# Attention kernel, one core: the order of score pairs from a table of words, and other first steps

## The reference, cut to what matters

```
q, k, v = (x @ Wqkv.T + bqkv) split into 16 heads
attn = softmax(q k^T / 4)
coh  = sigmoid(tanh([x, c] @ Wc1.T + bc1) @ Wc2.T + bc2)
mod  = attn * coh / (sum(attn * coh) + 1e-8)
mod  = 0.79 * mod + 0.21 * fa            (fa: softmax over tokens, one row per batch)
x    = x + (mod @ v) @ Wout.T + bout
out  = x + quaternion_map(x)             (linear in x, per feature group)
```

## Time and profile before

| | |
|---|---|
| median of 3 runs | 289.14 us (288.78 to 289.9) |
| the profiled execution | 288.7 us, its span 286.8 us |
| PE busy | 266.9 us, 93% |
| DVE busy | 193.1 us, 67% |
| ACT busy | 176.3 us, 61% |
| POOL busy | 177.4 us, 62%, nearly all of it before 132 us |
| chain that ended last | PE 78%, DVE 16%, issue 3% |

### The profile page before, as it was taken

The page is one execution under the profiler, slowest core; times in us unless marked ns, Lnnn a source line. Parts: engine busy times, 40 slices in busy tenths (PEclk is TensorE's granted clock), DMA queues, the critical chain, the costliest instruction groups (busy, mean ns, idle before and its releaser), DMA issues.

```text
span 286.8 us, 4339 instructions
## 1 busy us (share of the span) xinstructions
PE 266.9 (93%) x1579; PEld 128.1 (45%) x1579; DVE 193.1 (67%) x219; ACT 176.3 (61%) x214; POOL 177.4 (62%) x162
## 2 busy tenths in 40 slices
PE   8999979989799999999999999999999788899963
PEld 7447533334344444445444544455444333362422
DVE  6377867776776767776777677766877688763223
ACT  3334357666777676766587686755677767656760
POOL 4993999999999999994030599991000899600000
PEclk9999999999999999999999999999999999999999
DMA  6813411521710020146600000335500001011002
GB/s 220 255 74 115 180 41 56 186 93 32 263 41 0 5 71 3 61 185 215 231 9 2 1 2 1 127 143 204 154 0 3 1 5 37 1 36 41 0 2 73
DMA packets 16309, 22.73 MB, mean 79 GB/s; under 512 B 2392, under 2 KB 8408, under 8 KB 16288
## 3 DMA queue, kind: packets, MB, share of 16 engines
q1 hardware_dynamic: 15456, 21.77, 22.0%
q10 hardware_dynamic: 832, 0.69, 0.8%
HBM read 8.41 MB, written 2.11 MB: 37 GB/s over the span
## 4 chain that ended last, share of the span: by engine, by line
PE 78%; DVE 16%; issue 3%; ACT 1%; DMA 1%; POOL 0%; DVEq 0%; ACTq 0%; POOLq 0%
PE o_ps L1036 19%; PE job_ps L811 15%; PE pair_ps L1008 14%; DVE maxima L676 13%; PE pair_ps L1021 11%; PE job_ps L925 4%; PE job_ps L823 2%; PE pair_ps L811 2%; PE pair_ps L1043 2%; PE o_ps L823 1%; PE pair_ps L899 1%; PE job_ps L866 1%; DVE qk L692 1%; PE job_ps L883 1%; PE job_ps L873 1%
## 5 line engine op out<-in xcount | busy, mean ns | idle before, releaser
L676 DVE TENSOR_REDUCE maxima<-pair_ps 128x2 f32<-128x1024 f32 x128 | 155.5, 1222 | 58.6 <-PE pair_ps L1008 58.4
L520 ACT ACTIVATE probs<-pair_ps 128x1024 f32<-128x1024 f32 x128 | 130.7, 1025 | 59.9 <-PE pair_ps L1021 59.2
L1036 PE MATMUL o_ps<-probs,vals 128*32 128x512 f32 x512 | 68.2, 605 | 0.8 <-ACT probs L520 0.8
L1021 PE MATMUL pair_ps<-stack 64*128 64x512 f32 x256 | 56.3, 438 | 8.7 <-DVE maxima L676 7.0
L1008 PE MATMUL pair_ps<-stack 63*128 63x512 f32 x256 | 63.3, 491 | 0.3 <-DVE stack L683 0.3
L1008 PEld LDWEIGHTS pair_ps<-stack 63*128 63x128 f32 x256 | 23.9, 183 | 48.3 <-issue 39.6
L391 POOL TENSOR_TENSOR vals<-v_new,row 128x256 f32<-128x256 f32 x16 | 11.4, 733 | 40.2 <-ACT v_new L561 39.9
L1021 PEld LDWEIGHTS pair_ps<-stack 64*128 64x128 f32 x256 | 24.1, 184 | 26.6 <-DVE maxima L676 18.9
L493 POOL TENSOR_TENSOR prod<-amap,x_tok 128x1024 f32<-128x1024 f32 x12 | 28.6, 2385 | 0.4
L366 POOL TENSOR_TENSOR x_lo<-x_raw,x_hi 128x1024 fp32r<-128x1024 f32 x3 | 7.2, 2384 | 20.8 <-ACT x_hi L526 20.8
L1036 PEld LDWEIGHTS o_ps<-probs,vals 128*32 128x32 f32 x512 | 10.1, 108 | 20.9 <-issue 18.0
(11 more groups left out here) (139 smaller groups left out, 304.8 us busy)
## 6 DMA issues: line engine op xcount, KB each, us to landing
stack<-qk SPq DMA_DIRECT2D x90, 128.0 KB, 2.1
x_tok<-x SPq DMA_DIRECT2D x4, 512.0 KB, 3.8
out<-y SPq DMA_DIRECT2D x8, 256.0 KB, 2.2
x_raw<-xT SPq DMA_DIRECT2D x3, 512.0 KB, 5.0
fa_now<-fa_rows SPq DMA_DIRECT2D x4, 256.0 KB, 4.2
row<-rows SPq DMA_DIRECT2D x1, 544.0 KB, 5.9
x_raw<-xT ACTq DMA_DIRECT2D x1, 512.0 KB, 5.0
qk<-wdirT SPq DMA_DIRECT2D x2, 256.0 KB, 3.6
```

The lines of the kernel that those rows point to most:

```text
L520: nc.scalar.activation(probs[:, t % 4, :, :], ps[:, :, :], ACT.Exp, scale=SCALE).then_inc(exp_done, 1)
L676: nc.vector.tensor_reduce(maxima[:, gg % 2, :, pair, i], pair_ps[SLOT["S", u]][:, :, :], AX_X, ALU.max, negate=True).then_inc(s_reduced, 1)
L1021: ins = nc.tensor.matmul(pair_ps[SLOT["T", t]][:, a, :], stack[64 * a:64 * a + ROWS + 1, 1, p, j * P:(j + 1) * P], stack[64 * a:64 * a + R ...
L1036: ins = nc.tensor.matmul(o_ps[h * VW:(h + 1) * VW, :], vals[:, j, gg % G * HG + h, :], probs[:, (2 * k + h // 2) % 4, h % 2, :], start=(j ...
```

## The change

Three edits.

1. **The order.** The step counter is replaced by three lines of words (`FIRST`, `MIDDLE` twice, `LAST`), which PE, ACT and DVE walk. `S`, `T` and `W` count themselves up; a job's name has `+` or `-` where it belongs to the next or the last batch. `xh` is the high part of x on ACT. S and T mostly stand in runs of up to three with W's and jobs between the runs, two W's now and then in a row. The turns of the three PSUM tiles follow the new order. `LEAD` becomes 11 and the number of early jobs 17. `fore` moves behind the last `back1`.
2. **Warming.** Five matmuls 128 x 256 on all 128 rows replace ten 64 x 128; their operand is a part of `y` that DVE fills first.
3. **The first weights.** The columns of q and k are reordered on the host, so that `q0` and `k0` are one half; that half is loaded first, and ACT and DVE split it (POOL splits the other half). SP now waits for that half, not for the first half of `wdirT`, before it issues the later loads.

```diff
+MIDDLE = (
+    "S coh0 S T S coh1 T S xh+ S max3- W W T T S v1 S T T tok1- W T S T tok2- W T S max0 W T T S q0+ S S T back0- "
...
+def items():
+    table, count = [], {"S": 0, "T": 0, "W": 0}
+    for b, line in enumerate([FIRST] + [MIDDLE] * (B - 2) + [LAST]):
+        for word in line.split():
+            if word in count:
+                table.append((word, count[word]))
+                count[word] += 1
+            else:
+                table.append((word.rstrip("+-"), b + word.count("+") - word.count("-")))
+    return table
...
-            sp.dma_start(w_raw[:, :, 0:2 * E], qkv_w[:, :, 0:2 * E]).then_inc(ld_qk, 16)
-            sp.wait_ge(ld_dir, 16)
+            sp.dma_start(w_raw[:, :, 0:E], qkv_w[:, :, 0:E]).then_inc(ld_qk, 16)
+            sp.wait_ge(ld_qk, 16)
+            sp.dma_start(w_raw[:, :, E:2 * E], qkv_w[:, :, E:2 * E]).then_inc(ld_qk, 16)
...
-            split_weights(0, 0, 2 * E, ld_qk)
+            split_weights(0, E, 2 * E, ld_qk, 32)
...
             x_high(0)
+            act.wait_ge(ld_qk, 16)
+            nc.scalar.activation(w_hi[:, :, 0:E], w_raw[:, :, 0:E], ACT.Copy).then_inc(w_first_hi, 1)
...
+            nc.vector.memset(y[:, 1, 0, :], 1.0).then_inc(warm_done, 1)
             nc.vector.memset(stack[:, 1, 2:, :].bitcast(F32), 1.0).then_inc(ones_done, 1)
...
+            dve.wait_ge(w_first_hi, 1)
+            nc.vector.tensor_tensor(w_lo[:, :, 0:E], w_raw[:, :, 0:E], w_hi[:, :, 0:E].bitcast(F32),
+                                    ALU.subtract).then_inc(w_first_lo, 1)
...
+                if kind in ("q", "k") and n == 0:
+                    pe.wait_ge(w_first_lo, 1)
...
-            pe.wait_ge(pool_step, 2)
-            for n in range(10):
-                nc.tensor.matmul(pair_ps[0][:, 0, 0:P], n_ones[:, :], n_ones[:, :], start=True, stop=True)
+            pe.wait_ge(warm_done, 1)
+            for n in range(5):
+                nc.tensor.matmul(pair_ps[0][:, 0, 0:E], y[:, 1, 0, 0:P], y[:, 1, 0, :], start=True, stop=True)
...
+            for name, n in ITEMS:
+                if name == "S":
                     scores_for_max(n)
...
-    wqkv = np.concatenate([by_part(wqkv[:2 * E]), wqkv[2 * E:]])
+    parts = by_part(wqkv[:2 * E]).reshape(4, P, E)
+    wqkv = np.concatenate([parts[[0, 2, 1, 3]].reshape(2 * E, E), wqkv[2 * E:]])
```

More of the change, by code:

```diff
@@ L36 @@
 HALF_SLOTS = 3
[L39 to L49, removed]
 POOL_SPLIT = 2
 LATE = ("q0", "q1", "k0", "k1", "out0", "out1")
[L56 to L63, removed]
-    return table
@@ L67 @@
-JOBS = jobs_by_step()
-LAST_STEP = max(JOBS)
-ORDER = [(name, 0) for name in BEFORE] + [job for n in range(LAST_STEP + 1) for job in JOBS.get(n, [])]
+BEFORE = ["dq0", "dk0", "q0"]
+FIRST = (
[3 rows of a table added]
+MIDDLE = (
[3 rows of a table added]
+LAST = (
[4 rows of a table added]
+def items():
[7 more added lines that the diff above has]
+                table.append((word.rstrip("+-"), b + word.count("+") - word.count("-")))
+    return table
@@ L70 @@
+ITEMS = items()
+NOT_JOBS = ("S", "T", "W", "xh", "fore")
+ORDER = [(name, 0) for name in BEFORE] + [item for item in ITEMS if item[0] not in NOT_JOBS]
 PLACE = {job: n for n, job in enumerate(ORDER)}
[L73 to L86, removed]
@@ L89 @@
-EVENTS = events()
-ALONE = len(EVENTS) - LEAD
+EARLY = len(BEFORE) + len([item for item in ITEMS[:ITEMS.index(("T", 0))] if item[0] not in NOT_JOBS])
+EVENTS = [item for item in ITEMS if item[0] in ("S", "T")]
+LEAD = EVENTS.index(("T", 0))
+ALONE = EVENTS.index(("S", STEPS - 1)) + 1
 SLOT = {event: n % 2 if n < LEAD else (n - LEAD + 2) % 3 if n < ALONE else
@@ L108, in last_early, with last_use_of_x @@
     return ORDER[max(n for n in range(EARLY) if n % 4 == bank)]
+def last_use_of_x(b):
+    return max(((name, b) for name in ("k1", "v1", "coh1")), key=PLACE.get)
 ROW_BV, ROW_BOUT, ROW_Q, ROW_GATE, ROW_END = 0, 256, 512, 1024, 1088
@@ L355, in chain, with split_weights @@
                 pool.wait_ge(pool_step, count[0])
-            def split_weights(n, c0, c1, loaded):
-                pool.wait_ge(loaded, 16)
+            def split_weights(n, c0, c1, loaded, count):
+                pool.wait_ge(loaded, count)
                 nc.gpsimd.tensor_copy(w_hi[:, :, c0:c1], w_raw[:, :, c0:c1]).then_inc(w_split, 1)
@@ L524, in x_high @@
                 if b >= 2:
[L525 removed]
+                    wait_job(act, last_use_of_x(b - 2))
                 nc.scalar.activation(x_hi[:, b % 2], x_raw[:, :, :], ACT.Copy).then_inc(x_hi_done, 1)
@@ L657, in _ @@
                 evacuate((name, 0))
[L658 to L667, removed]
+            for name, n in ITEMS:
+                if name == "T":
+                    exponentials(n)
+                elif name == "W":
+                    if n % IT == IT - 1 and n // IT != G * B - 2:
+                        attention_out(n // IT)
+                elif name == "xh":
+                    x_high(n)
+                elif name not in NOT_JOBS:
+                    evacuate((name, n))
         @block.vector
@@ L787, in _ @@
                 direct_low((name, 0))
-            for n in range(LAST_STEP + 2):
-                if n < STEPS:
+            held = [("q0", 0)]
+            for name, n in ITEMS:
+                if name == "S":
                     reduce_scores(n)
[L791 to L797, removed]
-                        evacuate(job)
-                for job in JOBS.get(n, []):
-                    if job[0] not in LATE:
-                        evacuate(job)
+                    for job in held:
+                        evacuate(job)
+                    held = []
+                elif name == "W":
+                    if n == IT * (G * B - 1) - 1:
+                        attention_out(n // IT)
+                elif name in LATE and ITEMS.index((name, n)) < ITEMS.index(("S", STEPS - 1)):
+                    held.append((name, n))
+                elif name not in NOT_JOBS:
+                    evacuate((name, n))
         @block.tensor
@@ L831, in project @@
                 pe.wait_ge(x_lo_done, b + 1)
-                pe.wait_ge(w_split, {"q": 2, "k": 2, "v": 4, "coh": 6}[kind])
+                if kind in ("q", "k") and n == 0:
+                    pe.wait_ge(w_first_lo, 1)
+                else:
+                    pe.wait_ge(w_split, {"q": 2, "k": 2, "v": 4, "coh": 6}[kind])
                 if kind == "v":
@@ L839, in project @@
                 else:
-                    c0 = {"q": 0, "k": E, "coh": 3 * E}[kind] + n * P
+                    c0 = 3 * E + n * P if kind == "coh" else n * E + (P if kind == "k" else 0)
                     ins = split_product(bank(job), lambda a, k: w[a][:, k, c0:c0 + P],
@@ L1046, in _ @@
                 run_job((name, 0))
-            for n in range(LAST_STEP + 1):
-                if n < STEPS:
+            for name, n in ITEMS:
+                if name == "S":
                     scores_for_max(n)
[L1050 to L1055, removed]
+                elif name == "T":
+                    scores(n)
+                elif name == "W":
+                    weigh_values(n)
+                elif name == "fore":
                     output_fore()
-                for job in JOBS.get(n, []):
-                    run_job(job)
+                elif name not in NOT_JOBS:
+                    run_job((name, n))
 def kernel(x, cond_256, L0_cond_Wqkv, L0_cond_bqkv, L0_cond_Wout, L0_cond_bout, L0_cond_Wc1, L0_cond_bc1,
```

6 lines of the change are left out of this document (3 added, 3 removed), and 9 rows, old and new, of tables (FIRST, LAST, MIDDLE).

## The result

The changed kernel takes 262.62 us (median of 4 runs, 262.36 to 262.73), the kernel before 289.52 in the same sitting (4 runs, 288.78 to 291.64): ratio 0.905, 95% interval 0.901 to 0.909. The forecast was 269.3 with a range of 264 to 278. The profiled execution took 262.61 us, its span is 260.8 against 286.8: 26.0 us less, where the sum said 19.8.

A forecast was written before the change was run, and what follows sets the result against it. PE was taken as the bound, its time split into prices by kind and waits for PSUM tiles. Gains of 5.6, 14.8, 1.7 and 1.4 less 2.3, 0.4 and 1 sum to 19.8: 289.14 to 269.3 us, range 264 to 278.

The forecast's parts named there:

- fewer runs: PE's order: 131 runs of pairs become 106 at 0.20 each, 63 runs of W become 57: 5.6 us gained.
- slot waits: PE's S and T waiting for a PSUM tile cost 15.5 us; the new order leaves 0.7: 14.8 gained.
- `zt`: PE's wait of `zt` for the low part of `k0` goes, as `zt` now stands later: 1.7 us gained.
- start: Warming on all rows raises PE's clock sooner, so the first S comes at 12.1: 1.4 us gained.
- POOL: PE reaches W 16 at 96.1, POOL's values come at 98.4, so PE waits there: 2.3 us lost.
- end with `fore`: Last W's wait shortened, 0.6 gained; `fore` moved into the 0.93 idle before the output, 1.0 lost: net -0.4 us.
- chance waits: New waits because DVE and ACT are fuller: 1 us deducted, bounds 0 and 5.
- A: Rival at the start: the clock rises no sooner, first S at about 14.2, 271.5 us; chance 0.11.
- B: Rival: a third pair in a run costs 0.34, not 0.23, over 62 runs of three: 275.5 us; chance 0.08.
- C: Rival: half the slot waits come back elsewhere, through DVE's jobs or W's exponentials; 7.4 lost, 276.7 us; chance 0.19.
- D: Rival: slower, as each of 62 runs of three waits 0.5 for tiles, 31 us: 298 us; chance 0.05.
- E: Rival: no change, PE's gain ends at something outside PE, such as later POOL values for W 16; chance 0.03.

The follow-up runs named there:

- reductions over an eighth: Maxima reduced over one eighth of the keys, nothing else differing: 272.42 us on the kernel before, 263.17 us on the changed kernel.
- start alone: The kernel before, in its old order, with the new warming and first-weights start: 287.85 us, ratio 0.993.
- POOL's order changed: Changed kernel with the third batch's `x_lo` and the second batch's first `values` one mapping step earlier in POOL's list: 260.06 us.
- the cuts: Changed kernel with runs of pairs cut: 13 runs of three, third pair moved behind `tok` or `back`, 266.79 us; nine runs at small jobs, 265.84 us.
- order alone: Changed kernel with the start of before: ten warming matmuls on 64 rows, all first weights split on POOL: 264.77 us.
- nine cuts: Changed kernel with nine runs of pairs cut at small jobs (`max`, `z`, `field`), no `tok`, `back` or W moved: 265.84 us.

## Why the prediction was right in most of its mechanisms and wrong in its size

| term of the sum, us | forecast | measured | from |
|---|---|---|---|
| fewer runs | 5.6 | 6.4 | what the other terms leave of 23.5 |
| slot waits | 14.8 | 16.6 | reductions over an eighth: 17.4 before, 0.8 after |
| `zt` | 1.7 | 1.7 | its wait is gone |
| start | 1.4 | 2.5 | first S 13.41 and 10.92; start alone 2.4 |
| POOL | -2.3 | -3.0 | POOL's order changed |
| end with `fore` | -0.4 | 1.8 | `fore` last in the kernel before |
| chance waits | -1 | 0 | small waits of PE for ACT and the maxima's DMA: 0.9 before, 0.8 after |
| sum | 19.8 | 26.0 | spans 286.8 and 260.8 |

*What bounds the kernel*: the prices by kind and the tiles that DVE frees late held, with 0.23 to 0.24 in a run and 0.90 for three. *Fewer runs* is the one row that is a rest and not a measurement; 25 runs at the 0.19 to 0.32 of the cuts are 4.8 to 8, and six W's that now follow another save 0.15 each, 0.9, which holds it.

*Slot waits* failed in size, by 1.8. The step "The pair that waited then costs 0.43 to the next kind and not 0.33, 33 x 0.10 = 3.3 more" counted only places where the T's spacing was visibly late; the trace has 4.8 there, over 47 places, 21 of them (2.2 us) behind a T that was not late. And "the six places that fall short add up to 0.7" came out at 0.8 in all. The needs worked out for S T S (1.5) and T S T (1.2) were enough.

*The end* failed as a step, not only in size, by 2.2. "`fore` moves into the only idle place left there [...], 1.0 lost. Net -0.4" priced `fore` at its new place and never at its old one. There PE had no idle time to give, so the 1.9 that left the middle was a gain by itself. At its new place it cost 0.64 and not 1.0; with the last W's 0.65 regained the tail came out even.

*The start* was right in what raises the clock and wrong by 1.1 on when, by about 0.7 if the average of the profiles is taken. "DVE's first instruction starts at 1.85" was read from a row in which that instruction is the large fill. The small fill ahead of it started at 0.84; 1.0 of idle time stood in front of the large fill, now at 2.13; what it waits for there, no run shows.

*POOL*: right place, 0.7 too small. PE was ready for W 16 some 1.8 sooner than the 96.1 of the forecast (94.33 with POOL's order changed), by what the other terms had too low, and POOL's values were 1.0 sooner than the 98.4 (97.42). (POOL's busy time before is not nearly all ahead of 132 us, as the table of before has it: 118.5 of 177.4 is.) *Chance waits* of 1 were set aside for nothing.

Of the rivals, A (the clock rises no sooner) is out: 64 rows cost 1.9 us. B (0.34 for a third pair) is out: 58 of the 62 third pairs start 0.23 to 0.26 after the second, as the 0.24 at 92.35. C (half of the slot waits come back) is out by the 0.8. D and E have no row that speaks for them; D's 298 adds its 31 us to the span of 267.0, and as a median it would be 300.

## What to carry to other kernels

When work moves from a stretch where the bounding engine has no idle time into one where it waits, price both ends of the move: the old place gives back the full duration, the new one costs only what sticks out of the wait. Size a wait for a buffer by taking it away in a copy of the kernel (here by reductions that finish early) instead of adding up visible gaps, because each gap also makes its neighbours dearer. And when one part of a change makes the bounding engine earlier, look for the queue that will then be late, here POOL's; a two-line change of its order was worth another 1%.

## What the runs showed of the hardware that was not expected

PE's clock can fall in a kernel that keeps PE busy for more than 93% of its span, after one wait. In the kernel before with `fore` last, the `zt` wait of 1.74 was followed by a stretch at the low level; busy time of each engine by stretch, then granted clock, DMA share, GB/s:

```profile
41.00:42.00 1.00, 0.00 (x0) 0.00 (x0) 1.00 (x2) 0.38 (x1) 0.91 (x2) 1.00 0.00 0
...
43.00:44.00 1.00, 1.00 (x6) 0.86 (x5) 1.00 (x1) 0.92 (x1) 0.94 (x6) 0.93 0.03 8
44.00:45.00 1.00, 1.00 (x3) 0.37 (x2) 0.08 (x1) 0.11 (x1) 1.00 (x7) 0.50 0.00 0
```

By 48 us that execution was 1.4 us behind the trace of before, where the same wait, just as long, left the clock at 1.00. The wait of `q0` for POOL did the same (0.50 from 88 to 91 us on) in three kernels in which it lasted 1.8 (order alone, and the changed kernel with shorter reductions), and not in the changed kernel, where it lasted 1.50. It cost them little, since W 16 then waited less. So a wait's price can be more than its length, and whether it is differs from execution to execution.

The times of the kernel before in the four sittings go with its mean granted clock: 26 runs at 0.999 or 1.000 took 288.4 to 289.8 us, six at 0.994 took 289.8 to 290.1, and sixteen at 0.980 to 0.993 took 291.0 to 291.9. Medians of few of its runs can thus differ by a microsecond and more.

The idle stretches ahead of the last outputs belong here too. Of the five kernels without a `fore` there, two ran the last outputs at 0.50 in their profile; of the eleven with one, none. That `fore` at the end protects the clock is thus likely and not shown, with one profiled execution of each.

An 8 KB transfer was late once behind a large one. In the kernel with nine cuts ACT issued the maxima's rows at 136.30, just behind a 512 KB load of tokens (136.12), and T had them at 140.75; in the changed kernel they went out at 135.62, ahead of that load (136.31), and T started at 138.71 without a wait. That the load is the cause is likely and not shown.
